# First cross attention of a two-layer perceiver kernel: value products of four head groups in one batch, value projection in two halves

## The reference

```python
q = x @ Wq.T;  k_raw = context @ Wk.T;  v_raw = context @ Wv.T
q = q.reshape(b, n, NHEADS, HEAD_DIM).transpose(0, 2, 1, 3)
kv = jnp.concatenate([k_raw, v_raw], axis=-1).reshape(b, m, NHEADS, HEAD_DIM, 2)
k, v = kv[..., 0].transpose(0, 2, 1, 3), kv[..., 1].transpose(0, 2, 1, 3)
q, k = _rmsnorm(q), _rmsnorm(k)
attn = jax.nn.softmax(jnp.einsum('bhnd,bhmd->bhnm', q, k) * scale, axis=-1)
out = jnp.einsum('bhnm,bhmd->bhnd', attn, v)
```

## Time and profile before

| | us |
|---|---|
| median of 3 runs (1568.25 to 1570.9) | 1569.55 |
| the profiled execution, device time | 1574.83 |
| its span in the trace | 1573.0 |
| the first cross attention's 64 bodies, in the trace | 43.5 to 446.8 |
| granted clock of TensorE, mean over the span | 0.949 |

### The profile page before, as it was taken

One profiled execution on the slowest core, in us unless ns is written; L12 is line 12 of the kernel. 1 busy time (PEld: TensorE's weight loads), 2 busy tenths in 40 slices (PEclk: granted clock), 3 DMA queues, 4 the chain that ended last, 5 costly groups with the idle time before them and its releaser, 6 DMA issues. The chain is left out here.

```text
span 1573.0 us, 32445 instructions
## 1 busy us (share of the span) xinstructions
PE 1435.9 (91%) x11879; PEld 1095.3 (70%) x11884; DVE 1038.9 (66%) x1731; ACT 772.0 (49%) x1135; POOL 158.7 (10%) x103
## 2 busy tenths in 40 slices
PE   4999999999979899999938999996999788899998
PEld 3666666666635389999927877773666355789997
DVE  5666656666623488888784778776999542576664
ACT  2777777777722354444322222325888303365552
POOL 0000000000011233333321111210000010000000
PEclk8999999999989989999959999996999868899999
DMA  4333334333240164444134232315888030476662
GB/s 149 76 85 88 84 87 82 80 80 80 47 127 1 39 225 178 166 167 171 47 134 134 95 133 93 129 72 123 177 176 170 8 91 3 162 256 218 217 212 74
DMA packets 128101, 186.19 MB, mean 118 GB/s; under 512 B 73987, under 2 KB 91091, under 8 KB 124564
## 3 DMA queue, kind: packets, MB, share of 16 engines
q1 hardware_dynamic: 128036, 185.30, 40.7%
HBM read 149.14 MB, written 17.47 MB: 106 GB/s over the span
## 5 line engine op out<-in xcount | busy, mean ns | idle before, releaser
L465 ACT ACTIVATE x_probs<-psum 128x1024 f32<-128x1024 f32 x256 | 248.6, 1030 | 4.2 <-PE psum L353 3.0
L175 PE MATMUL psum<-m_x_hi,m_gu_hi 128*128 128x256 f32 (+1 forms) x816 | 232.3, 285 | 5.4 <-DVE m_h L2277 2.8
L176 PE MATMUL psum<-m_x_hi,m_gu_lo 128*128 128x256 f32 (+1 forms) x816 | 231.3, 284 | 0.0
L177 PE MATMUL psum<-m_x_lo,m_gu_hi 128*128 128x256 f32 (+1 forms) x816 | 230.9, 283 | 0.0
L175 PE MATMUL psum<-x_w_hi,x_ctx_hi 128*128 128x256 f32 (+1 forms) x640 | 212.3, 332 | 11.7 <-DVE x_ctx_lo L492 11.7
L176 PE MATMUL psum<-x_w_hi,x_ctx_lo 128*128 128x256 f32 (+1 forms) x640 | 195.3, 305 | 0.0
L177 PE MATMUL psum<-x_w_lo,x_ctx_hi 128*128 128x256 f32 (+1 forms) x640 | 194.9, 305 | 0.0
L1475 DVE TENSOR_REDUCE x_peaks<-psum 128x2048 f32 (+1 forms) x64 | 146.3, 2290 | 61.8 <-PE psum L1391 61.8
L175 PEld LDWEIGHTS psum<-x_w_hi,x_ctx_hi 128*128 128x128 f32 x640 | 121.9, 190 | 76.2 <-issue 61.1
L175 PEld LDWEIGHTS psum<-m_x_hi,m_gu_hi 128*128 128x128 f32 (+1 forms) x816 | 152.1, 186 | 8.4 <-DVE m_h L2277 3.3
L176 PEld LDWEIGHTS psum<-m_x_hi,m_gu_lo 128*128 128x128 f32 (+1 forms) x816 | 152.1, 186 | 1.2
(11 more groups left out here) (305 smaller groups left out, 2511.6 us busy)
## 6 DMA issues: line engine op xcount, KB each, us to landing
m_gu_raw<-in_m_gu SPq DMA_DIRECT2D x18, 1408.0 KB, 6.1
m_gu_raw<-in_m_gu SPq DMA_DIRECT2D x32, 768.0 KB, 4.3
x_k_stack<-x_keys_dram SPq DMA_DIRECT2D x45, 512.0 KB, 7.0
x_ctx_raw<-in_ctxT SPq DMA_DIRECT2D x64, 256.0 KB, 2.7
m_dn_raw<-in_m_down SPq DMA_DIRECT2D x16, 768.0 KB, 4.3
m_dn_raw<-in_m_down SPq DMA_DIRECT2D x18, 512.0 KB, 3.9
x_ctx_raw<-in_ctxT SPq DMA_DIRECT2D x16, 512.0 KB, 3.9
x_keys_dram<-x_keys_hi SPq DMA_DIRECT2D x16, 512.0 KB, 3.2
```

Of the source, the lines that this page charges most:

```text
L175: pe.matmul(out, a[0], b[0], start=start, stop=False, skip_group_check=True)
L176: pe.matmul(out, a[1], b[0], start=False, stop=False, skip_group_check=True)
L177: return pe.matmul(out, a[0], b[1], start=False, stop=stop, skip_group_check=True)
L465: act.activation(probs[:, grp, :], g.psum[:, 2 + 2 * (grp % 2):4 + 2 * (grp % 2), :].rearrange("p b n -> p (b n)"), ACT.Exp).then_inc(prob ...
```

## The change

`probs` becomes a pair of buffers, the second of which is the memory of `w_raw`; even bodies use the first, odd bodies the second. With that `exps(grp)` of body n waits only for W of body n - 2 (`pv_done`), but must not begin in body 1 before `w_raw` has been split. `v_part` moves out of the bank that it shared with `k_part` into another, and the wait for `k_copied` ahead of V goes. On TensorE the body's order is now S of groups 0 and 1; K; the first half of V (chunks 0 and 1, 6 matmuls); S of groups 2 and 3; W of groups 2 and 3 of the body before and of groups 0 and 1 of this body, one after the other; the second half of V (6 matmuls). No matmul is added or removed.

```diff
-        probs = sb("probs", [P, HG, 4 * L], F32)
+        probs = [sb("probs", [P, HG, 4 * L], F32), w_raw]
...
-        k_part, v_part = kv_bank[:, 0:HW], kv_bank[:, HW:2 * HW]
+        k_part, v_part = kv_bank[:, 0:HW], spare_bank[:, HW:2 * HW]
...
-                def values(s, half, out):
-                    for c in range(NC):
+                def values(s, half, out, cs=range(NC)):
+                    for c in cs:
                         last = project(s, c, out, half * D + HW)
-                    last.then_inc(v_projected, 1)
+                        if c == NC - 1:
+                            last.then_inc(v_projected, 1)
...
-                                         vals[:, s % 2, 4 * grp + q, :], probs[:, grp, at:at + L],
+                                         vals[:, s % 2, 4 * grp + q, :], probs[s % 2][:, grp, at:at + L],
...
                     for grp in (0, 1):
                         score(n, s, half, grp)
+                    if at + 3 < STEPS:
+                        pe.wait_ge(k_copied, n + 3)
+                        if at + 3 == MT:
+                            pe.wait_ge(w_split, 2 * NC)
+                        keys(n + 3, (s + 3) % SLOTS, half_of(at + 3), k_part)
+                    pe.wait_ge(vals_ready, n + 1)
+                    if at + 1 < STEPS:
+                        values((s + 1) % SLOTS, half_of(at + 1), v_part, range(NC // 2))
+                    for grp in (2, 3):
+                        score(n, s, half, grp)
                     if at:
                         for grp in (2, 3):
                             weigh(n - 1, (s + 3) % SLOTS, grp)
-                    if at + 3 < STEPS:
-                        pe.wait_ge(k_copied, n + 3)
-                        pe.wait_ge(vals_ready, n + 1)
-                        if at + 3 == MT:
-                            pe.wait_ge(w_split, 2 * NC)
-                        keys(n + 3, (s + 3) % SLOTS, half_of(at + 3), k_part)
-                    for grp in (2, 3):
-                        score(n, s, half, grp)
                     if at == MT:
                         pe.wait_ge(acc_taken, 2)
                         clear()
-                    pe.wait_ge(vals_ready, n + 1)
                     for grp in (0, 1):
                         weigh(n, s, grp)
                     if at + 1 < STEPS:
-                        if at + 3 < STEPS:
-                            pe.wait_ge(k_copied, n + 4)
-                        values((s + 1) % SLOTS, half_of(at + 1), v_part)
+                        values((s + 1) % SLOTS, half_of(at + 1), v_part, range(NC // 2, NC))
...
                         act.wait_ge(scores_ready, 4 * n + grp + 1)
-                        act.wait_ge(pv_done, 4 * n + grp + 1)
-                        act.activation(probs[:, grp, :],
+                        if at:
+                            act.wait_ge(pv_done, 4 * n + grp - 3)
+                        act.activation(probs[s % 2][:, grp, :],
...
+                    if at == 1:
+                        act.wait_ge(w_split, 2 * NC)
                     exps(0)
                     exps(1)
```

## The result

| | before | changed |
|---|---|---|
| median (16 runs each) | 1570.2 us | 1566.4 us |
| ratio to before, 95% interval | | 0.9976 (0.9966 to 0.9987) |
| the profiled execution, device time | 1574.83 | 1565.44 |
| first cross attention, first S of body 0 to the last W's end | 403.3 | 399.8 |

The change is faster by 3.8 us (2.0 to 5.3). The prediction had -4.7 and 1564.9 from a median of 1569.55, with a range of 1562.0 to 1570.0. The two profiled executions differ by more, 9.4 us, but only 3.5 of that lies in the stage that was changed. Two profiles of the kernel before, which is the same program, differ by 4.5 us outside the stage and by 0.2 inside it. So I read the stage in the traces, and the whole program only in medians.

What follows compares the result with a forecast made beforehand. TensorE, busy 136.00 of 136.00 us at full clock, was taken as the bound. Terms -8.1 - 1.3 + 3.0 + 0.8 + 0.3 + 0.6 = -4.7 us put the median at 1564.9 from 1569.55, range 1562.0 to 1570.0.

Steps and rivals of the forecast that it cites:

- 58 inner bodies: Bodies 2 to 31 and 33 to 60: 6.18 us instead of 6.32, 0.14 saved each, -8.1 us (-5.8 to -9.9).
- late transposes: Two TensorE waits in the stage, 1.0 and 1.06 us: keys squared earlier give back 0.5 and 0.8, -1.3 (0 to -2.1).
- start, to body 2: Body 1: exponentials wait for the split of w_raw and TensorE stands; body 2 begins at 58.55, not 55.58: +3.0 (2.8 to 3.3).
- body 32: VectorE's accumulator copy loses the cover of K and S; body 32 takes 7.7 us: +0.8 (0.6 to 1.3).
- bodies 61, 62, without the late transpose: Bodies without K, held by the exponentials: body 62 becomes 5.51 from 5.37, as does 61: +0.3.
- body 63: Last body: six groups of W in a row end at 5.53 after its start instead of 4.89: +0.6.
- The joint of S and P: Inner body, S then P: 0.57 us, bounds 0.54 and 0.61; rival at 0.61, 1567.1, 15%; at 0.54, 1563.0, 12%.
- the batch changes buffer and accumulator: Rival for W in inner bodies: this switch costs a joint, four groups take 1.98, body 6.31, median 1572.4; 3%.
- ScalarE's slack: Inner bodies: 0.5 us ahead of S of group 3, so no TensorE wait; rival that ScalarE falls behind, 7%.
- a clock under 1 behind 55: Stated sign that the prediction is wrong: the clock showing less than 1 behind 55, after the stall in body 1.
- a rival at 8%: The stall in body 1 brings the clock down, losing 1.7 us: sum -3.0, median 1566.6; 8%.
- Its upper corner: Upper bounds of all gains added: -8.4 us, 1561.2, left outside the range.

Runs made afterwards that it cites:

- W apart: Changed kernel with the early split, W in two batches again, before and behind S of groups 2 and 3: ratio 0.9982, inner body 6.31 us.
- V whole: Changed kernel with the early split, the whole value projection behind the merged W instead of half ahead of S of groups 2 and 3: ratio 0.9989.
- old order: Kernel before plus the pair of exponential buffers and ScalarE's wait for the weight split, TensorE's order as before: ratio 1.0033, stage 409.5 us.
- body 32: Changed kernel, but in body 32 alone W of body 31 stands right behind S of groups 0 and 1: ratio 0.9967, body 32 6.84 us.
- control: Changed kernel with TensorE's bodies 1 to 4 written out instead of being the hardware loop's first round: ratio 0.9984, body 1 11.34 us.
- the one with 1.65 and 0.52: Changed kernel, VectorE splitting two of four chunks of the second half's weights behind context tile 2, the others in body 0: ratio 0.9967.
- the wait filled: Changed kernel with TensorE's bodies 1 to 4 written out and 22 matmuls of zeros in body 1's wait: ratio 0.9955, body 1 9.79 us.
- early split: Changed kernel, VectorE splitting the second half's weights right behind context tile 2 instead of in body 0: ratio 0.9937, stage 395.6 us.
- early split, 32 and 61 to 63: Changed kernel with the early split and, in bodies 32 and 61 to 63, the previous body's W behind S of groups 0 and 1: ratio 0.9928.

## Why the prediction was right, step by step

| term | predicted | measured in the stage |
|---|---|---|
| 58 inner bodies | -8.1 (0.14 each) | -7.8 (0.133 each) |
| late transposes | -1.3 | -2.1 (1.01 and 1.06, both gone) |
| start, to body 2 | +3.0 | +4.65 |
| body 32 | +0.8 | +0.9 |
| bodies 61, 62, without the late transpose | +0.3 | +0.2 |
| body 63 | +0.6 | +0.65 |
| sum | -4.7 | -3.5 |

- **The body** was 6.19 for 6.18. The joint of S and P showed as 0.54 until P begins and 2.35 for P, 2.89 together, where I had 0.57 and 2.31. So the 0.61 of body 0 was not the bare joint. W merged to 1.85 on the dot; that the batch changes buffer and accumulator costs nothing. W apart shows that this, not the order as such, is the gain.
- **ScalarE's slack** held, and V whole shows how narrow it is: S of groups 2 and 3 0.72 earlier, and the gain is gone.
- **The transposes** were undersized. I took them as partly chance and gave back 1.3 of 2.07.
- **The start** is the term that was off, by 1.65, and by one of the prediction's own signs of being wrong, a clock under 1 behind 55, this step was wrong: it had the stall at full clock. The stall itself was as worked out: with the clock held, body 1 took 9.79 where my sum has 9.68. The 0.1 between them is that ScalarE began 0.21 after the split's end (53.86 to 54.07), for which I had 0.1. The other 1.55 is the clock. I had its fall as a rival at 8%, with 1566.6 for the median, closer to the measured 1566.4 than the forecast proper. It fell in all four traces that have this stall: changed, old order, body 32, control. It did not in the one with 1.65 and 0.52, nor with the wait filled.
- **The evidence for the 8%** was a single gap of 2.82 us that the clock outlasted, and that was too little. The second wait of 0.52 is not what makes the difference: with body 32 changed, the clock fell at 55.30, 2.56 us into the first wait and before any more work. Two windows ahead of the matmuls that end this wait show it:

```profile
54.80:55.30 0.50, 0.00 (x0) 0.00 (x0) 0.50 (x2) 0.50 (x1) 0.00 (x0) 1.00 0.00 0
55.30:55.50 0.20, 0.00 (x0) 0.00 (x0) 0.20 (x2) 0.20 (x2) 0.00 (x0) 0.50 0.00 0
```

```profile
55.59 0.61 PE L354 MATMUL psum<-x_q_rows,x_keysT 64*128 64x256 f16 x4 [2.85 <-ACT x_w_raw L469]
```

In the old order it fell at 54.66, 2.20 us into the wait of 2.56. Nor does the length of a gap decide by itself. A gap of 2.43 us later in the program, in code that no kernel here changes, is in all twelve traces. In nine the clock is at 1.00 for the 3.2 us behind it, in two (early split, control) at 0.50, and in one (early split, 32 and 61 to 63) it fell 1.4 us behind the gap. Here are the matmuls behind the gap and the window from their start, first of the kernel before, then of the early split:

```profile
1235.56 0.66 PE L1704 MATMUL psum<-ident,x_oT 128*128 128x128 f32 x4 [2.43 <-ACT x_sT L1691]
1235.60:1238.80 3.20, 1.93 (x16) 1.70 (x16) 2.04 (x7) 0.00 (x0) 0.00 (x0) 1.00 0.01 3
```

```profile
1227.26 1.12 PE L1706 MATMUL psum<-ident,x_oT 128*128 128x128 f32 x4 [2.43 <-ACT x_sT L1693]
1227.20:1230.40 3.20, 3.14 (x15) 3.15 (x16) 1.01 (x3) 0.00 (x1) 0.00 (x0) 0.50 0.03 10
```

What decides in such a case stays open. So the fall in body 1 is shown for this stall, and one trace with 1.65 and 0.52 doesn't show that a stall of that size is safe. The Trainium skill ("TensorE: Matmul & The Clock Gate", Why this matters for your kernels) warns of idle gaps, though of longer ones than either wait here: it named the mechanism, and the traces show it at shorter gaps.
- **Luck.** The two wrong sizes point against each other (+1.65, -0.8), which is part of why the total came within 1 us. The range was wide enough to hold the clock's rival as well. Its upper corner is misadded, too: the best cases that the prediction states give -7.7 and 1561.9, not -8.4 and 1561.2.

## What to carry to other kernels

- On a saturated TensorE count the joints between kinds of work, not only the matmuls: here a batch of column-strip products that is interrupted once less per body is worth 0.12 us, 7 us in 58 bodies, if the engine that feeds it keeps its slack; check that slack in the new order, since it was 0.5 us and 0.72 would have spent it.
- A buffer that is reused has a last reader. Look when that reader runs in the first body and move it into its engine's idle time: that was worth 4.2 us in the stage, more than the change as it stood.
- A batched order that is right in the loop can be wrong where it is uncovered. The body that takes the accumulators and the last bodies wanted the old order, 2.8 us together.
- Don't rule out a fall of the clock because one gap of that length didn't bring it down. Look at the same gap in several traces, or price both cases.

## What the runs showed of the hardware

A stall costs more than its length when the clock falls: 3.4 us of waiting (2.85 and 0.52) brought 3.4 us at a granted clock of 0.50, which is the level of 1.2 GHz, and another 1.55 us of time. In the trace of the kernel with only body 32 changed the same stall brought 6.8 us at 0.50, and 2.6 us of time (12.38 against 9.79). The clock fell as early as 2.20 and 2.56 us into a wait, and held through other gaps of 2.43 and 2.82 us. 22 matmuls of zeros into an unused part of a bank held the clock at 1.00.

From the last pass of column strips to the first full-array matmul it is 0.33 us where a pass takes 0.22, so this joint costs 0.11. For the sum over a body it hardly matters which kind follows which: six joints in the new order gave 6.31, six in the old 6.32.
